# Issuing the attention scores of two heads together, on the two halves of TensorE's rows

## The reference

```python
xn = _layernorm(x, axis=-1)                    # x: (2, 16384, 1024) f32
s  = _L0_attn_ref(xn, ...)
g  = _silu(_L0_ffn_ref(xn, w_gate, w_up, w_down))
x  = x + s * g

# _L0_attn_ref, windowed differential attention: H=16 heads of D=64, G=2 key groups, W=256
q1, q2 = x @ Wq1, x @ Wq2                      # per head; k1, k2, v: per group; rope on q and k
sc = einsum('bhnqd,bhnkd->bhnqk', qw, kw) * scale       # windows of 256, one every 128 positions
p  = softmax(sc, axis=-1)
a  = attn(q1, k1, v) - lam * attn(q2, k2, v)
return a.reshape(...)[:, :L] @ Wout + bout
```

## Time and profile before

| | us |
|---|---|
| median of 2 runs | 2736.57 (2729.5 to 2743.64) |
| the profiled execution | 2733.13 |
| its span on the slowest core | 2731.7 |
| spans of the 8 cores | 2712.2 to 2731.7 |
| attention, first score matmul to the end | 1835.3 to 2731.7 |

### The profile page before, as it was taken

The page is one execution under the profiler, slowest core; times in us unless marked ns, Lnnn a source line. Parts: engine busy times, 40 slices in busy tenths (PEclk is TensorE's granted clock), DMA queues, the critical chain, the costliest instruction groups (busy, mean ns, idle before and its releaser), DMA issues.

```text
span 2731.7 us, 33992 instructions; the slowest of 8 cores (2712.2 to 2731.7 us)
## 1 busy us (share of the span) xinstructions
PE 2169.2 (79%) x9479; PEld 943.0 (35%) x9479; DVE 968.6 (35%) x2369; ACT 1171.1 (43%) x1937; POOL 209.1 (8%) x225
## 2 busy tenths in 40 slices
PE   3355899999899999898922666668888888888887
PEld 2232444444344444343411222223333333333332
DVE  2233212121212121211033233336665666566654
ACT  3354232222313131411134211127776777677764
POOL 1110000000000000000000222220000100010001
PEclk9999999999999999999955899986666766676666
DMA  8993424242424242423281000013211121112110
GB/s 151 162 152 124 139 100 138 101 131 94 138 93 147 93 147 94 145 85 123 77 199 47 1 0 1 0 28 80 78 47 47 59 81 47 47 58 82 47 47 31
DMA packets 74484, 236.53 MB, mean 87 GB/s; under 512 B 10434, under 2 KB 10435, under 8 KB 74052
## 3 DMA queue, kind: packets, MB, share of 16 engines
q1 hardware_dynamic: 50324, 172.52, 18.6%
q0 software_dynamic: 15024, 28.28, 7.4%
q10 hardware_dynamic: 8960, 33.56, 3.9%
HBM read 214.24 MB, written 46.14 MB: 95 GB/s over the span
## 4 chain that ended last, share of the span: by engine, by line
PE 28%; ACT 13%; issue 4%; DVE 4%; ACTq 1%; DVEq 0%; POOLq 0%
PE ps_p L673 5%; PE ps_w L969 5%; ACT pe_sb L856 4%; PE ps_a L881 4%; PE ps_w L960 3%; ACT rz_sb L891 3%; ACT rz_sb L896 3%; PE ps_r L920 2%; PE ps_s L846 2%; ACT qf L681 2%; PE ps_s L841 2%; PE ps_ra L710 1%; PE ps_a L876 1%; PE ps_vt L627 1%; ACT xa_tm L616 1%
## 5 line engine op out<-in xcount | busy, mean ns | idle before, releaser
L385 PE MATMUL ps_gu<-xn_fm,wgut 128*128 128x512 bf16 x1536 | 366.0, 381 | 84.5 <-DVE h_sb L406 41.8
L406 DVE TENSOR_TENSOR h_sb<-ps_gu,silu_g 128x512 bf16<-128x512 f32 x192 | 130.8, 690 | 563.1 <-ACT silu_g L401 563.1
L393 PE MATMUL ps_gu<-xn_fm,wgut 128*128 128x512 bf16 x1344 | 323.5, 381 | 0.0
L401 ACT ACTIVATE silu_g<-ps_gu,zbias 128x512 bf16<-128x512 f32 x192 | 129.9, 687 | 449.5 <-PE ps_xt L340 339.4
L856 ACT ACTIVATE pe_sb<-ps_s,ubias 128x512 bf16<-128x512 f32 x512 | 319.7, 674 | 5.3 <-PE ps_s L841 2.1
L881 PE MATMUL ps_a<-pe_sb,v_tm 128*65 128x256 bf16 (+1 forms) x768 | 184.4, 369 | 84.9 <-ACT rz_sb L896 82.0
L891 ACT ACTIVATE rz_sb<-ps_a,zbias 1x512 f32<-1x512 f32 x256 | 173.4, 677 | 175.6 <-PE ps_a L876 172.2
L385 PEld LDWEIGHTS ps_gu<-xn_fm,wgut 128*128 128x128 bf16 x1536 | 140.0, 97 | 261.5 <-issue 117.1
L904 DVE CAST asb_e<-ps_a 64x512 bf16<-64x512 f32 x256 | 176.0, 688 | 148.7 <-PE ps_a L876 145.4
L896 ACT ACTIVATE rz_sb<-rz_sb,zbias 1x512 bf16<-1x512 f32 x256 | 184.2, 719 | 25.2 <-ACT rz_sb L891 1.9
L393 PEld LDWEIGHTS ps_gu<-xn_fm,wgut 128*128 128x128 bf16 x1344 | 132.2, 98 | 161.0 <-issue 4.3
(11 more groups left out here) (122 smaller groups left out, 2468.7 us busy)
## 6 DMA issues: line engine op xcount, KB each, us to landing
wgut<-scr_gu SPq DMA_DIRECT2D x192, 512.0 KB, 3.4
xc<-x_ffn SPq DMA_DIRECT2D x32, 512.0 KB, 4.5
scr_g<-g_stage ACTq DMA_DIRECT2D x32, 512.0 KB, 2.6
g_tm<-scr_g ACTq DMA_DIRECT2D x16, 1024.0 KB, 6.5
x_win<-x_ffn SPq DMA_DIRECT2D x16, 1024.0 KB, 10.5
out<-o_stage SPq DMA_DIRECT2D x16, 1024.0 KB, 8.4
scr_gu<-stag SPq DMA_DIRECT2D x48, 256.0 KB, 5.1
xa_f<-x_attn SPq DMA_DIRECT2D x17, 512.0 KB, 6.0
```

What stands on the lines that cost most here:

```text
L385: e.matmul(ps_gu[par][:], wt[:, k, :], fm[:, k, :], start=(k == 0), stop=(k == 7)))
L393: e.matmul(ps_gu[2 + par][:], wt[:, 8 + k, :], fm[:, k, :], start=(k == 0), stop=last)))
L406: e.tensor_tensor(h_sb[:, m, :], ps_gu[2 + par][:], silu_g[par][:], ALU.mult).then_inc(sV.h, 1))
```

## The change

The eight score matmuls of an even head and the odd head after it are issued together, in the even slot. The order is `p`, then key chunk, then head, so matmuls on rows 0 to 63 and on rows 64 to 127 alternate. The odd slot issues no score matmuls. The wait for free banks now covers both heads: for head `s + 1` it is the exponential of head `s - 1`, which ACT has in the slot just before. One increment of PE's semaphore for each `p` stands for both heads. The exponentials stay where they were, one slot each.

```diff
-                def emit_F(hh):
-                    n, h = divmod(hh, H)
-                    hp = hh % 2
-                    c, po = h // 2, (h % 2) * 64
+                def emit_scores_pair(s):
                     for p in range(2):
                         qbuf = q1r if p == 0 else q2r
                         kbuf = k1r if p == 0 else k2r
-                        if hh >= 2:
-                            em.wait("tensor", (sC.h, s2p[(hh - 2, p)]))
+                        for x in (s, s + 1):
+                            if x >= 2:
+                                em.wait("tensor", (sC.h, s2p[(x - 2, p)]))
                         for kc in range(2):
-                            last = kc == 1
-                            em.add("tensor", ...
-                        s1_done[(hh, p)] = sT.inc()
+                            for x in (s, s + 1):
+                                n, h = divmod(x, H)
+                                c, po = h // 2, (h % 2) * 64
+                                last = kc == 1 and x == s + 1
+                                em.add("tensor", lambda e, q=qbuf, k=kbuf, n=n, kc=kc,
+                                       po=po, c=c, p=p, hp=x % 2, last=last:
+                                       (e.matmul(ps_s[hp][p][:, kc * 256:(kc + 1) * 256],
+                                                 k[po:po + 64, 128 * (n + kc):128 * (n + kc) + 128],
+                                                 q[po:po + 64, c, 128 * n:128 * n + 256],
+                                                 start=(kc == 0), stop=(kc == 1)).then_inc(sT.h, 1)
...
+                        tok = sT.inc()
+                        s1_done[(s, p)] = tok
+                        s1_done[(s + 1, p)] = tok
+
+                def emit_F(hh):
+                    hp = hh % 2
+                    if hh % 2 == 0:
+                        emit_scores_pair(hh)
                     for p in range(2):
                         em.wait("scalar", (sT.h, s1_done[(hh, p)]))
```

More of the change, by code:

```diff
@@ L850, in emit_F @@
-                        s1_done[(hh, p)] = sT.inc()
+                            for x in (s, s + 1):
[8 more added lines that the diff above has]
+                                                 start=(kc == 0), stop=(kc == 1)).then_inc(sT.h, 1)
+                                        if last else
+                                        e.matmul(ps_s[hp][p][:, kc * 256:(kc + 1) * 256],
+                                                 k[po:po + 64, 128 * (n + kc):128 * (n + kc) + 128],
+                                                 q[po:po + 64, c, 128 * n:128 * n + 256],
+                                                 start=(kc == 0), stop=(kc == 1))))
```

## The result

| | before | after |
|---|---|---|
| median, us | 2743.64 (2727.92 to 2889.59, 11 runs) | 2760.91 (2752.77 to 2853.43, 12 runs) |
| ratio to before | | 1.0102, 95% interval 1.0076 to 1.0128 |
| the profiled execution: span, us | 2731.7 | 2765.1 |
| spans of the 8 cores | 2712.2 to 2731.7 | 2733.1 to 2765.1 |
| attention, first score to the end, per core | 896.4 to 899.8 | 915.5 to 925.5 |

Both sides ran interleaved on the same chip; some executions of either kernel are long because a die was disturbed, and the ratio leaves them out. The attention is the steadier measure: it differs by 3.4 us between the cores of before, and it holds the change.

What follows compares the result with a forecast made beforehand. Plain slots were bound by the loop reciprocal, V, logarithm, reciprocal (2.79 us), tail slots by PE. Savings of 3.7 - 0.4 + 3.0 = 6.3 us from a median of 2736.6 gave 2730 us, range 2714 to 2746.

Steps and rivals of the forecast that it cites:

- Plain slots at nothing, side by side: In slots without tail groups, paired scores overlap, ending 0.03 to 0.05 us later against 0.49 us spare on PE: no cost.
- The rival of serial scores: Both heads' scores run one after the other, V starts 0.45 us late in even plain slots: 2774 us, chance 5%.
- The added wait and the shared increment at nothing: PE's wait for the previous slot's exponentials and ACT's wait for both heads' scores of one `p` cost nothing.
- Tail 1 earlier by 3.7 us in all: In tail 1's odd slot without scores, 11 windows save 0.14 us each and the first four save 0.53 each.
- tail 3 by 3.0: In tail 3's odd slot without scores, the group starts 0.20 us earlier in each of 15 windows.
- tail 2 later by 0.4: In tail 2's even slot, a pair instead of four score matmuls loses 0.03 us in each of 15 windows.
- the three rows: Trace readings that DVE's product takes 0.69 us and the next group starts 0.15 us after it, limiting tail 1 and 3.
- the rival of the full 15.9 us: DVE's product does not hold back tail 1 and tail 3, each gains 0.53 us per window: 2721 us, chance 6%.
- The sum: Tail slots together, 3.7 - 0.4 + 3.0, make the kernel 6.3 us shorter.
- the clock rival: New waits of some 0.3 us in two tail slots hold the clock down: 109 us, 2846 us at worst, chance 3%.
- a milder form: The moment of the clock's rise shifts by some 0.6 us per window, up to 9 us in total either way.
- The price: Each tail group at the half clock takes 5.22 instead of 2.79 us, 2.43 us more.

## Why the prediction was wrong

- *Plain slots at nothing, side by side:* right. Eight score matmuls take 1.03 us, the period is 2.80 us, V is not late. The rival of serial scores falls.
- *The added wait and the shared increment at nothing:* right. V starts 0.15 us after the reciprocal as before.
- *Tail 1 earlier by 3.7 us in all, tail 3 by 3.0, tail 2 later by 0.4:* 2.9, 3.0 and, in the windows that aren't late, 0.0. DVE's product holds the groups back as the three rows said, and the rival of the full 15.9 us falls. That 2.9 is near 3.7 is partly luck. I had taken the clock to rise where it did before. Now, on the slowest core, it rises 6.1 us or more after the start of tail 0, so every window but the first takes 6.65 us, the length at the half clock. The first four windows, which took 7.64 to 7.01, save 2.7 of it; the other eleven, which took 6.78 to 6.54, save 0.3 together and not 11 x 0.14.
- *The sum:* the terms give 6.3 and the measured savings 2.9 + 3.0 + 2.0 = 7.9 us, the 2.0 in the plain stretch being unforeseen. On top of that came 29.7 + 5.1 us, and this is the step that failed: **the clock rival**. I gave it 3% at its full price and a milder form at 9 us either way. I priced it as what *waits* do to the clock, found 0.3 us of waiting harmless beside the 1.01 of the earlier trace rows, and stopped. The waits are indeed no part of it: in the late windows PE is busy without a break. What matters is what was taken out: the change removed the scores between the groups of tail 0 and tail 1, the only work there beside V with more than one row, in the very stretch in which the clock rises. With that one pair undone, or with matmuls of 64 rows in its place, the 65 late windows become 7 and 6. I had a hint in the rows: the earlier trace rows show that the clock rises at a varying moment in just that slot. I took the variation as noise of 9 us and not as a sign that each window stands near an edge.
- *The price:* a late group costs 7.78 - 4.15 = 3.6 us, more than the 2.43 that I took from tail 0, as V, R and the scores are slower too. Seven windows at that price and two at 2.2 us made the 29.7.
- *The Trainium skill:* "TensorE: Matmul & The Clock Gate", Why this matters for your kernels, asks for TensorE to be kept busy continuously, without long idle gaps. By that the clock should have been up in this stretch. The trace doesn't agree: PE is busy for 6.65 of 6.65 and 7.78 of 7.78 us with the clock at 0.50 and 0.51, and the measurement decides. The Trainium skill's "TensorEngine Tiling (Array Packing)", PSUM Bottleneck, was right in what I took from it (tail 3 waits 0.26 us for the product), but it spoke of the smaller effect.

## What to carry to other kernels

Where the granted clock changes within a stage, ask of each edit what it takes from the stretch ahead of a rise, and look at the rows of contraction that work there, not only at PE's busy time: with one row in the four filling matmuls 108 of 120 windows were late, with 64 rows 6, and PE was as busy in both. A kernel that repeats can settle into a rhythm with the clock in which savings of a few tenths of a microsecond vanish; measure an edit there by its stretches and on all cores before believing a ratio near 1. And idle time that an edit makes is worth something here only when something is moved into it: the same pairs cost 1.0% as they were made and gave 1.9% once the tail stood in the slot they had emptied and the one-row bias was short.

## What the runs showed of the hardware beyond what I expected

- With PE busy without a break for 14 us (tail 0 to tail 2: 6.65 + 7.78), the clock was at its half level (0.50 and 0.51). The stretch held f32 and bf16 matmuls with one row for about 2 x 2.04 (bias) and 2 x 0.60 us (R) of it.
- With four filling matmuls of 256 columns between the two groups, the late windows go with their rows: 108 of 120 with one row, 6 with 64, none with 128.
- Two heads on the two halves of the rows seem to count for more than one: with the tail one slot later, no late window in 120 with a pair in the slot of tail 1, and 37 with one head. The two kernels differ in their other slots too, so this is not shown by itself.
- Cores of one chip with the same program fall into different rhythms: the kernel with one pair at tail 1 ran the attention in 991.5 to 1001.5 us on seven cores and in 933.3 on the eighth.
